# A twelve-stage perceiver megakernel on one core: earlier weight splits in stage 2, and a new placing of fetches, jobs and small sums in stage 9

## What is computed

```python
x = x + L0_xattn(layernorm(x), ctx, mask)       # stage 0
x = x + L0_attn(layernorm(x))                   # stage 1, linear attention and an MLP
x = x + L0_ffn(layernorm(x))                    # stage 2, 256 -> 1024 -> 1024 -> 1024 -> 256
...
x = x + L3_xattn(layernorm(x), ctx, mask)       # stage 9
x = x + L3_attn(layernorm(x))                   # stage 10
x = x + L3_ffn(layernorm(x))                    # stage 11

# L3_xattn: 16 heads of 16 columns
q = split_heads(h @ q_w.T + q_b); k = split_heads(ctx @ k_w.T + k_b); v = split_heads(ctx @ v_w.T + v_b)
scores = einsum('bhqd,bhkd->bhqk', q, k) / sqrt(16);  scores = where(mask, -inf, scores)
out = einsum('bhqk,bhkd->bhqd', softmax(scores), v)
```

## Time and profile before

| | |
|---|---|
| runs | 1467.9, 1468.68, 1463.27 us, median 1467.9 |
| profiled execution | 1463.04 us, its span 1460.9 us |
| TensorE busy | 1386.2 us (95% of the span) |
| VectorE busy | 981.6 us (67%) |
| ScalarE busy | 797.0 us (55%) |
| GpSimd busy | 362.6 us (25%) |
| TensorE's share of the chain that ended last | 72%, VectorE 15%, ScalarE 4%, GpSimd 3%, DMA 3%, issue 2% |
| largest group | L2397, VectorE's reductions of stage 9: 256 of 1222 ns, 306.8 us |

### The profile page before, as it was taken

The page is one execution under the profiler, slowest core; times in us unless marked ns, Lnnn a source line. Parts: engine busy times, 40 slices in busy tenths (PEclk is TensorE's granted clock), DMA queues, the critical chain, the costliest instruction groups (busy, mean ns, idle before and its releaser), DMA issues.

```text
span 1460.9 us, 24247 instructions
## 1 busy us (share of the span) xinstructions
PE 1386.2 (95%) x9599; PEld 986.7 (68%) x9609; DVE 981.6 (67%) x1627; ACT 797.0 (55%) x1453; POOL 362.6 (25%) x461
## 2 busy tenths in 40 slices
PE   7799989999999999999999989999999998999997
PEld 5788657887898676898566654555555554645797
DVE  5776655334787576787367567989999983566433
ACT  5575335343665364664455426878888885315232
POOL 3685263001633113542101222222121100100000
PEclk9999999999999999999999999999999999999999
DMA  9313215334222433211317174444545304210140
GB/s 373 142 58 130 106 42 179 105 110 176 80 73 109 169 119 123 96 59 57 145 71 263 61 239 165 141 160 131 182 138 174 111 2 187 86 59 1 59 173 15
DMA packets 49071, 177.76 MB, mean 122 GB/s; under 512 B 4864, under 2 KB 6144, under 8 KB 43008
## 3 DMA queue, kind: packets, MB, share of 16 engines
q1 hardware_dynamic: 48960, 176.23, 33.7%
HBM read 132.66 MB, written 44.60 MB: 121 GB/s over the span
## 4 chain that ended last, share of the span: by engine, by line
PE 72%; DVE 15%; ACT 4%; POOL 3%; DMA 3%; issue 2%; SPq 0%; ACTq 0%; POOLq 0%; DVEq 0%
PE PS L160 50%; DVE SM L2397 8%; PE PS L2382 5%; PE PS L2286 4%; PE PS L630 2%; PE PS L2300 2%; DMA CT<-k_tiles 2%; PE PS L1874 1%; PE PS L1895 1%; POOL CNr L1342 1%; PE PS L2961 1%; PE PS L1902 1%; PE PS L2866 1%; DMA k_tiles<-CN 1%; DVE ARr L2414 1%
## 5 line engine op out<-in xcount | busy, mean ns | idle before, releaser
L2397 DVE TENSOR_REDUCE SM<-PS 128x1 f32<-128x1024 f32 x256 | 306.8, 1222 | 31.9 <-PE PS L2286 29.5
L160 PE MATMUL PS<-ARr 128*128 128x256 f32 (+1 forms) x1024 | 271.2, 336 | 0.6 <-POOL CNr L928 0.5
L160 PE MATMUL PS<-CNr,ARr 128*128 128x256 f32 (+1 forms) x952 | 202.1, 320 | 11.7 <-DVE ARr L797 11.4
L160 PEld LDWEIGHTS PS<-ARr 128*128 128x128 f32 x1024 | 181.1, 190 | 18.9 <-issue 0.7
L160 PEld LDWEIGHTS PS<-CNr,ARr 128*128 128x128 f32 x952 | 154.1, 194 | 26.6 <-DVE ARr L797 13.1
L160 PE MATMUL PS<-ARr,HTr 128*128 128x512 f32 x384 | 121.7, 398 | 0.5 <-ACT CN L459 0.5
L2286 PE MATMUL PS<-ARr 64*128 64x512 f32 x320 | 117.1, 448 | 5.1 <-ACT AR L2469 2.8
L858 ACT CAST ARr<-PS 128x512 fp32r<-128x512 f32 x96 | 56.3, 586 | 113.4 <-PE PS L630 113.4
L2300 PE MATMUL PS<-ARr 64*128 64x256 f32 x640 | 116.5, 304 | 1.3 <-DVE ARr L2414 1.0
L2469 ACT ACTIVATE AR<-PS 128x512 f32<-128x512 f32 x172 | 93.5, 605 | 23.4 <-PE PS L2300 14.0
L2469 ACT ACTIVATE CT<-PS 128x512 f32<-128x512 f32 x168 | 91.2, 602 | 18.6 <-PE PS L2300 15.3
(11 more groups left out here) (412 smaller groups left out, 2799.0 us busy)
## 6 DMA issues: line engine op xcount, KB each, us to landing
CT<-k_tiles SPq DMA_DIRECT2D x64, 512.0 KB, 5.0
CN<-ctx_n SPq DMA_DIRECT2D x24, 1024.0 KB, 5.7
k_tiles<-CNr SPq DMA_DIRECT2D x32, 768.0 KB, 3.5
CT<-pack SPq DMA_DIRECT2D x6, 2048.0 KB, 7.6
CT<-ctx_t SPq DMA_DIRECT2D x8, 1024.0 KB, 19.5
k_tiles<-CN SPq DMA_DIRECT2D x32, 256.0 KB, 4.1
AR<-pack SPq DMA_DIRECT2D x16, 512.0 KB, 3.5
v_ones<-CN SPq DMA_DIRECT2D x28, 288.0 KB, 3.2
```

Source lines behind the costliest of these rows:

```text
L160: last = te.matmul(o, l, r, start=first and k == 0, stop=final and k == n - 1, skip_group_check=True)
L2397: ve.tensor_reduce(MX9[:, p % 2, e, g % 2, g % 8 // 2:g % 8 // 2 + 1], PS[:, b:b + 2, :].rearrange("p a b -> p (a b)"), AX, ALU.max).then_inc(
```

## The change

Six edits. In stage 9: (1) the job lists: "s9" has 6 jobs (k v k v v v) instead of 10, and "heads" 9 (k v k v k v k v k), of which the value jobs stand in step 8p + 5; (2) SyncE and GpSimd do quarters 4 to 6 in the start steps, for n < 3, and quarter n // 2 + 6 at even steps n of the pairs; (3) `turn_rows` adds the transposed maxima of all 128 partitions and 256 columns to the query tile in one instruction; (4) the sum of `finish` onto x moves from VectorE to GpSimd; (5) its input t9 has two buffers, so VectorE waits for the sum before last. In stage 1: (6) `weights_pool_1` is called at the opening of `pool_1`.

```diff
--- before.py
+++ after.py
@@ -390,7 +390,7 @@
                              ("h3", "v"), ("b4", "kv"), ("t4", "k"), ("b5", "kvk"), ("t5", "v"), ("h5", "v"),
                              ("b6", "kkkk"), ("t6", "k"), ("h6", "v"), ("b7", "kvk"), ("t7", "v"),
                              ("s7", "v"), ("b8", "kvkv"), ("t8", "k"), ("r8", "v"), ("b9", "vvk"),
-                             ("t9", "k"), ("s9", "kvvkvvvvvv"), ("heads", "k" * 5)):
+                             ("t9", "k"), ("s9", "kvkvvv"), ("heads", "kvkvkvkvk")):
             JOBS[place] = []
             for kind in kinds:
                 JOBS[place].append((kind, upto[kind]))
@@ -1155,6 +1155,7 @@
 
         def pool_1(pl):
             ge = pl.e
+            weights_pool_1(pl)
             pl.wait_ge(*w1)
             ge.tensor_tensor(W1["pb"], W1["pb"], W1["gamma"], ALU.mult).then_inc(*pl.inc("row", "pbg", 1))
             ge.tensor_tensor(W1["c2b"], W1["c2b"], W1["gamma"], ALU.mult).then_inc(*pl.inc("row", "c2g", 1))
@@ -1169,7 +1170,6 @@
             for i in range(4):
                 pl.wait_ge(("xy", 1, i), ("c2g", 1))
                 ge.tensor_tensor(Y1[:, i, :], Y1[:, i, :], W1["c2b"], ALU.add).then_inc(*pl.inc("row", "xyb", 1, i))
-            weights_pool_1(pl)
             jobs_pool(pl, "t1b")
             pl.end(1)
 
@@ -2187,7 +2187,7 @@
         sm_begin()
         s9_rs = sm(4)
         MX9, ri9 = sm(2, 2, 2, 4), sm(2, 2, 2)
-        t9 = sm(2, 2, 16)
+        t9 = [sm(2, 2, 16) for _ in range(2)]
 
         QQ9 = view(ARr, 0, 8, 512)
 
@@ -2212,6 +2212,8 @@
         jobs, PAIR_JOBS = list(JOBS["heads"]), {}
         for p in range(5):
             PAIR_JOBS[8 * p + 1] = jobs.pop(0)
+            if jobs:
+                PAIR_JOBS[8 * p + 5] = jobs.pop(0)
         assert not jobs
 
         def start_steps():
@@ -2409,9 +2411,9 @@
             def turn_rows(p):
                 _, pr, cols = of_pair(p)
                 dv.wait_ge(("row_ps", 9, p), ("qm", pr))
-                for e in range(2):
-                    r = slice(64 * e + 32, 64 * e + 33)
-                    ve.tensor_copy(QQ9[r, pr, cols], bank("rows", p)[r, 0:256]).then_inc(*dv.inc("turn", "mrow", 9, p))
+                rows = QQ9[:, pr, cols]
+                ve.tensor_tensor(rows, bank("rows", p)[:, 0:256], rows.bitcast(F32), ALU.add).then_inc(
+                    *dv.inc("turn", "mrow", 9, p))
 
             turn_out(dv, 9, "ht", HT, 0)
             for m in range(2):
@@ -2436,15 +2438,11 @@
                 if what == "finish":
                     b2, pr, _ = of_pair(n)
                     ps = bank("fin", n)[:, 0:68].rearrange("p (i e r) -> p i e r", i=2, e=2)
-                    x = X[:, 2 * b2:2 * b2 + 2, 32 * pr:32 * pr + 32]
                     dv.wait_ge(("fin_ps", 9, n), ("fin_out", 9, n - 1) if n else None)
                     ve.reciprocal(ri9[:, n % 2], ps[:, :, :, 16]).then_inc(*dv.inc("mixed", "ri", 9, n))
-                    dv.wait_ge(("ri", 9, n), ("fin", 9, n - 1) if n else ("row", 9, 3))
-                    ve.tensor_tensor(t9, ps[:, :, :, 0:16], ri9[:, n % 2].unsqueeze(3).to_broadcast([128, 2, 2, 16]),
+                    dv.wait_ge(("ri", 9, n), ("fin", 9, n - 2) if n > 1 else None)
+                    ve.tensor_tensor(t9[n % 2], ps[:, :, :, 0:16], ri9[:, n % 2].unsqueeze(3).to_broadcast([128, 2, 2, 16]),
                                      ALU.mult).then_inc(*dv.inc("mixed", "fin_out", 9, n))
-                    dv.wait_ge(("fin_out", 9, n))
-                    ve.tensor_tensor(x, x, t9.rearrange("p i e r -> p i (e r)"), ALU.add).then_inc(
-                        *dv.inc("mixed", "fin", 9, n))
                     if n == 15:
                         x_done(dv, 9, 2, ("fin", 9, n))
                         x_done(dv, 9, 3, ("fin", 9, n))
@@ -2502,13 +2500,19 @@
                 keys_pool(pl, i)
             for n, job in enumerate(JOBS["s9"]):
                 job_pool(pl, *job)
-                if n < 8:
+                if n < 3:
                     keys_pool(pl, 4 + n)
             for what, n, k in pair_steps():
-                if what in ("beside", "both") and n % 2 == 0 and n and k == 0 and n // 2 + 11 < 64:
-                    keys_pool(pl, n // 2 + 11)
+                if what in ("beside", "both") and n % 2 == 0 and n and k == 0 and n // 2 + 6 < 64:
+                    keys_pool(pl, n // 2 + 6)
                 if what == "job":
                     job_pool(pl, n, k)
+                if what == "finish":
+                    b2, pr, _ = of_pair(n)
+                    x = X[:, 2 * b2:2 * b2 + 2, 32 * pr:32 * pr + 32]
+                    pl.wait_ge(("fin_out", 9, n), ("fin", 9, n - 1) if n else ("row", 9, 3))
+                    pl.e.tensor_tensor(x, x, t9[n % 2].rearrange("p i e r -> p i (e r)"), ALU.add).then_inc(
+                        *pl.inc("mixed", "fin", 9, n))
             pl.end(9)
 
         W10, w10_load = placed("s10", CTf, 4096, None, "Wo")
@@ -2557,14 +2561,14 @@
             jobs_sp(sp, "b9", "t9", kinds="k")
             for n, job in enumerate(JOBS["s9"]):
                 job_sp(sp, *job)
-                if n < 8:
+                if n < 3:
                     fetch(sp, 4 + n)
             for what, n, k in pair_steps():
 
                 if what == "beside" and n == 37 and k == 0:
                     fixed_rows(sp, 1)
-                if what in ("beside", "both") and n % 2 == 0 and n and k == 0 and n // 2 + 11 < 64:
-                    fetch(sp, n // 2 + 11)
+                if what in ("beside", "both") and n % 2 == 0 and n and k == 0 and n // 2 + 6 < 64:
+                    fetch(sp, n // 2 + 6)
                 if what == "job":
                     job_sp(sp, n, k)
                 if what == "mix" and n // 16 == 7:
```

## The result

The changed kernel took a median of 1490.6 us beside 1465.6 for the kernel before on the same chip: a ratio of 1.0162, 95% interval 1.0127 to 1.0197. The profiled execution's span grew from 1460.9 to 1488.2, by 27.3 us. The prediction was 1486 (1468 to 1505), slower.

The account below looks back on a forecast made before the run. TensorE was taken to set the pace in stage 9's pairs, VectorE having 0.1 us to spare. The terms sum to +20.3 us, giving 1483.3 from 1463.04 and 1488.2 from 1467.9; the middle, 1486, was forecast, range 1468 to 1505.

Parts of the forecast that it names:

- splits: Opening of stage 2: with its weight splits moved to stage 1's opening, TensorE's idle there shrinks; -5.9 us (-4.4 to -6.5).
- start of stage 9: Opening of the pairs: fewer jobs and fetches leave ScalarE's two waits without a cause; -11.8 us (-9.0 to -12.5).
- four value jobs: Stage 9's pairs: value jobs moved there take TensorE time, 4 x 1.9 us, +7.5 us (up to 8).
- five key stalls: Step 8p+4 of pairs 0 to 4: TensorE waits for a quarter fetched behind the key store; +20.4 us (16 to 25).
- value-job waits: Step 8p+8, after value jobs at 8p+5: quarter ready after 9.6 us against 9.0, four times; +1.6 us (0 to 4.4).
- pair 7: Stage 9's pair 7: fetches among second-batch value loads go out two steps ahead, three waits of 1 us; +3 us (0 to 5).
- clock dips: Behind the five stalls in pairs 0 to 4: TensorE's clock falls, 1.6 us each; +8 us (0 to 15).
- one sum: Max rows in the pairs: one sum replaces two casts, TensorE's wait for the second cast goes, fourteen times; -2.8 us.
- residual sum: Sum moved to GpSimd: only the last is on the path, into stage 10's norm; +0.3 us (0 to 0.5).
- Rival C: Step 8p+4 of pairs 0 to 4: the quarter is there in time, so no stalls; -12.7 us, 1453; chance 0.13.
- rival B: Stage 9's pairs: stalls come, but the clock stays high and pair 7 hides its fetches; +9.3 us, 1475; chance 0.20.
- Rival E: Start of stage 9: a store or quarter 6 still holds the first pairs; +32 us, 1498; chance 0.05.

## Why the prediction was right, term by term

The sign and the mechanism held, and the time lay in the range. In spans the sum was +20.3 and the measurement +27.3; between the medians it was +25.0. The terms, in the prediction's order:

| term | predicted | measured | from |
|---|---|---|---|
| splits | -5.9 | -5.3 | VectorE at 230.06 and 224.78 |
| start of stage 9 | -11.8 | -10.3 | reductions 1 to 24 |
| four value jobs | +7.5 | +7.8 | 24.57 against 22.64, 27.63 against 25.64 in pair 0 |
| five key stalls | +20.4 | +19.5 | five idles |
| value-job waits | +1.6 | +0.6 | one idle, at 985.08 |
| pair 7 | +3 | +8.5 | 29.31 against 20.78 |
| clock dips | +8 | +10.4 | warming products, less that idle |
| one sum | -2.8 | -3.4 | that edit alone |
| residual sum | +0.3 | +0.1 | 2.14 and 2.28 |
| unchanged code | 0 | -1.1 | other places of low clock |

The measured column sums to +26.8; 0.5 of the 27.3 is not assigned. It is about what the stalls cost in the pairs' periods beyond the idles themselves (20.2 against 19.5).

**The stalls** are the step that decided, and it held in all its links: place (step 4 of pairs 0 to 4), cause (SyncE's order, shown by the edit of that order alone) and size (4.24, 3.97, 3.67, 3.63, 4.02 against 4.8, 3.8, 3.8, 4.4, 3.6). The subtraction of one place in the queue from another, in the trace of before, was enough, because the job, split, store and fetch kept their distances. Rival C fell with that, and rival B too: it had the stalls without the dips. Rival E fell at the start, which gained what it should.

**The clock dips** were mis-sized, 1.6 instead of 2.4, 2.2, 2.2, 2.4 and 1.2 us. The estimate's 5.2 us of slow work, from the row at 219, were right for the first four: the low stretches are 6.8 us long, but begin inside the idle, and TensorE works 5.1 to 5.4 us of each; behind the fifth stall the stretch is 3.4. Wrong was what a microsecond of slow work costs: the key job gave 1 - 1.98/3.11 = 0.36, the pairs gave 0.42 to 0.46 behind the first four stalls and 0.36 behind the fifth. And the step down from 1.9 to 1.6, for stalls shorter than 4.43 us, wasn't borne out: the first four cost more than 1.9. The Trainium skill's TensorE: Matmul & The Clock Gate, section HAM oscillation, has matmuls that wait for a DMA in every round fall to the low clock in every round; five stalls and five dips agree, and the 9.5 us that the prediction worked out beside it were nearer to the 10.4 than its 8.

**Pair 7** is the term with the largest error, 3 against 8.5. Two idles of 1.75 and 2.45 us (4.2) against three of 1 us is the smaller part; no dip was given to them because 2.85 us of idle had left the clock alone, and both were followed by half clock. The other 4.3 us go with the dips: the runs with SyncE's order changed and with the products have idles of 4.6 and 4.4 us in this pair too, but one low stretch of 3.4 us instead of two of 3.4 and 6.8, and there the pair is 6.2 and 6.0 us longer than 20.78, 1.5 and 1.6 beside the idles. The source is the same as elsewhere: with one more quarter the pair takes 20.79. What was wrong was reading a lower bound for harmless idles from one row.

**The start** had nearly the right gain for a reason that was only half right. The prediction credited fresh value slots and the shorter fetch list together. The lead alone (37.28, all ten jobs and reused slots) and the moved jobs with a lead of eight steps (36.96) each give all of it. What held ScalarE in the kernel before was a value store landing late behind a fetch: it went out at 864.56, and ScalarE got its slot at 870.69, 6.1 us later; the other starts have 5.8 to 6.7 us with a fetch right ahead, 4.1 and 4.0 with none. The reuse of slots costs only when stores are late. So the four value jobs in the pairs, 7.8 us, buy nothing that the shorter lead had not given already. The 1.5 us short are not traced: the changed kernel's start has a stretch of low clock from 852.4 us on, but the lead-alone kernel has none there and takes as long. The start of the kernel before isn't the same in every execution either: in the runs with the splits alone and the sum alone, which leave it as it was, it took 48.47 and 48.44 us instead of 47.39, and pair 0 then 27.52 and 27.41 instead of 25.88; TensorE's second idle is 5.14 and 4.91 us there instead of 2.85, with half clock behind it. Against those two the start gives 11.3 us and pair 0 another 1.8.

**Value-job waits** came once in four. Timeline of the changed kernel at the value jobs of pair 0, without a wait, and of pair 3, with the one of 0.61 us:

```profile
883.23 1.99 PE L160 MATMUL PS<-CN,CT 128*128 128x256 f32 x8
...
886.24 0.93 SPq L2540 DMA_DIRECT2D CT<-k_tiles  x2
...
890.95 1.04 POOL L2553 CAST ARr<-CT 128x1024 fp32r<-128x1024 f32 x1 [11.86 <-DMA CT<-k_tiles]
...
978.37 1.10 SPq L2540 DMA_DIRECT2D CT<-k_tiles  x2
...
983.93 1.04 POOL L2553 CAST ARr<-CT 128x1024 fp32r<-128x1024 f32 x1 [12.39 <-PE PS L2302]
...
985.08 0.46 PE L2288 MATMUL PS<-ARr 64*128 64x512 f32 x1 [0.61 <-issue]
```

In pair 0 the copy starts 4.7 us after the fetch, not 5.4, and ends at 891.99, 8.8 us after the job's start: just under the 9.0 of the prediction. In pairs 1 and 2 it starts 4.8 and 5.0 us after it; in pair 3 5.6 us, and TensorE waits. (The arrow of that copy names score products; by the code it waits for those of pair 2, long done, and for the fetch.) The run with SyncE's order changed has such a wait of 0.45 us in pairs 1 and 3, which is where its periods of 25.11 and 25.08 come from.

**One sum** gave 3.4 instead of 2.8 because two periods gained more than the 0.2 of the others: 21.70 to 21.13 and 20.45 to 20.00. **The splits** came out within 0.6 us: the transposes start where TensorE's jobs end, as predicted, and the next thing late is ScalarE's and VectorE's copies, 1.22 us of idle. The add at the place they left fell from 1.08 to 0.43 us. At the place they went to, VectorE's normalizations slowed down, before and after:

```profile
154.74 1.38 DVE L299 TENSOR_SCALAR AR<-X,SM 128x256 f32<-128x256 f32 x4 [0.59 <-ACT SM L310]
...
159.31 0.87 DVE L1081 TENSOR_SCALAR HT<-PS,AR 128x128 f32<-128x128 f32 x3 [3.19 <-PE PS L345]
```

```profile
154.85 3.96 DVE L299 TENSOR_SCALAR AR<-X,SM 128x256 f32<-128x256 f32 x4 [0.56 <-ACT SM L310]
...
159.43 0.87 DVE L1081 TENSOR_SCALAR HT<-PS,AR 128x128 f32<-128x128 f32 x3 [0.62 <-PE PS L345]
```

The 2.6 us went into VectorE's wait behind them, 3.19 to 0.62; the row behind it stands 0.12 us later than before, as the first of them already did (0.11). The Trainium skill's GPSIMD Engine Reference, section Specifications, has GpSimd's SBUF interfaces shared with VectorE; the slower rows at both places agree with it. The microsecond that the prediction held ready for it didn't reach the path.

## What to carry to other kernels

In a queue that issues in program order, a transfer's lead is not the number of steps between its place and its use, but what is left of them after the slowest wait that stands before it; subtract these two times in the trace before shortening a lead. When a shorter lead pays for one thing (here late value stores) and costs another, move single entries of the queue before moving work between stages: one quarter of lead decided 40 us, most of it in the pairs, and one quarter's place 5.6 us in the start. A wait of several microseconds on TensorE should be priced with the slow stretch behind it.

## What the runs showed of the hardware

- A stall of 3.6 to 4.2 us on TensorE cost a further 1.2 to 2.4 us by half clock behind it; fourteen products of 3.19 us laid into it kept the clock at 1.00 and took all of that away.
- The length of one idle doesn't tell whether the clock falls: after 1.75 and 2.45 us it fell in pair 7 of the changed kernel, after 1.96 us in the same pair with SyncE's order changed it did not, nor after 2.85 us at 884.22 in the kernel before.
- A fetch of 512 KB took 6.1 to 6.4 us to GpSimd's copy right behind the 1 MB of key stores (5.0 in pair 4), 4.7 to 5.6 behind a value store, 3.9 with no store right ahead (882.12, lead alone); a value store with a fetch right ahead of it held its buffer for 5.8 to 6.7 us, and 4.0 to 4.1 without.
- Beside GpSimd's casts and differences four of VectorE's normalizations of 128x256 took 3.96 us instead of 1.38, and an add of two SBUF tiles 1.08 instead of 0.43.
